# Attention stack on one core: sums one step later, two multiply-adds for the values, the shift in five GpSimd steps, 128 rows in the first stage

## The reference

```python
q = _fq_sym(q, axis=-1); k = _fq_sym(k, axis=-1); v = _fq_sym(v, axis=2)   # 127 levels
attn = jnp.einsum('bhqd,bhkd->bhqk', q, k)
attn = jax.nn.softmax(attn, axis=-1)
attn = _fq_unsigned(attn, axis=-1)         # s = max(attn) / 255; round(attn / s) * s
out = jnp.einsum('bhqk,bhkd->bhqd', attn, v)
return out @ Wp + bp
```

## Time and profile before

| | |
|---|---|
| time, median of 3 runs | 4641.71 us (4641.0 to 4643.88) |
| the profiled execution: its time, its span | 4639.28 us, 4636.2 us |
| TensorE, VectorE, ScalarE, GpSimd busy | 96%, 87%, 76%, 80% |
| first stage | 0 to about 730 us |
| heads 0 to 14 | about 730 to 3972 us, 226 us the first, then about 215 us each |
| last head, epilogue | to about 4197 us, to the end |
| TensorE's mean granted clock | 0.982 |

### The profile page before, as it was taken

How to read it: one execution, slowest core, us unless ns; L and a number is a source line. 1 busy time by engine, 2 the same in 40 slices (tenths; PEclk the granted TensorE clock), 3 DMA queues, 4 the chain that set the end, 5 groups by cost and what they waited for, 6 DMA issues and landing times. The chain is left out here.

```text
span 4636.2 us, 150451 instructions
## 1 busy us (share of the span) xinstructions
PE 4459.4 (96%) x54175; PEld 1971.5 (43%) x54175; DVE 4037.1 (87%) x7370; ACT 3531.4 (76%) x3643; POOL 3692.6 (80%) x4025
## 2 busy tenths in 40 slices
PE   7999998999999999999999999999999999888999
PEld 5666663333333333333333333333333333224665
DVE  6788888999999999999999999999999999774333
ACT  3555557889889898989898988989898989873121
POOL 5777776899999999999999999999999999772000
PEclk9999997999999999999999999999999999998999
DMA  3555542111111111111111111111111111442010
GB/s 101 150 164 161 171 148 66 35 35 33 35 33 34 35 34 35 33 34 34 33 35 35 32 36 33 34 35 35 34 33 35 34 33 32 144 155 91 0 38 8
DMA packets 222771, 268.77 MB, mean 58 GB/s; under 512 B 34366, under 2 KB 202809, under 8 KB 221289
## 3 DMA queue, kind: packets, MB, share of 16 engines
q1 hardware_dynamic: 167529, 203.57, 15.8%
q10 hardware_dynamic: 54528, 55.60, 3.8%
HBM read 174.57 MB, written 82.97 MB: 56 GB/s over the span
## 5 line engine op out<-in xcount | busy, mean ns | idle before, releaser
L1546 ACT ACTIVATE e_home<-ps_scores,sk 125x896 f32<-125x896 f32 x3072 | 3076.2, 1008 | 388.7 <-ACTq L1545 204.3
L1579 DVE TENSOR_REDUCE unit_max<-ps_maxima 128x1 f32<-128x428 f32 (+2 forms) x5760 | 3115.2, 607 | 54.4 <-DVEq L1576 40.9
L1764 POOL TENSOR_SCALAR r<-e_home 125x896 f32<-125x896 f32 x2976 | 2769.6, 954 | 287.1 <-ACT e_home L1546 114.7
L1349 PE MATMUL ps_maxima<-e_home,unit 125*17 125x224 f32 x24576 | 1705.7, 354 | 12.2 <-PEq L1333 7.6
L1321 PE MATMUL ps_maxima<-k_home,q 48*128 48x428 bf16 (+2 forms) x5760 | 1614.8, 350 | 15.8 <-issue 1.8
L1293 PE MATMUL ps_scores<-q,k_home 54*128 54x448 bf16 x5760 | 1592.7, 356 | 4.8 <-PEq L1468 2.9
L1341 PE MATMUL ps_maxima<-r,vt 125*16 125x224 f16 x12288 | 854.5, 267 | 60.8 <-PEq L1335 30.7
L1293 PEld LDWEIGHTS ps_scores<-q,k_home 54*128 54x128 bf16 x5760 | 329.6, 95 | 1064.0 <-issue 1034.7
L1341 PEld LDWEIGHTS ps_maxima<-r,vt 125*16 125x16 f16 x12288 | 300.3, 86 | 783.0 <-issue 780.7
L1349 PEld LDWEIGHTS ps_maxima<-e_home,unit 125*17 125x17 f32 x24576 | 620.0, 95 | 19.2 <-issue 17.0
L1321 PEld LDWEIGHTS ps_maxima<-k_home,q 48*128 48x128 bf16 x5760 | 524.2, 93 | 233.3 <-issue 63.7
(11 more groups left out here) (270 smaller groups left out, 2723.6 us busy)
## 6 DMA issues: line engine op xcount, KB each, us to landing
k_rows<-krows ACTq DMA_DIRECT2D x48, 1000.0 KB, 7.0
k_home<-k_rows SPq DMA_DIRECT2D x408, 93.8 KB
k_home<-k_rows SPq DMA_DIRECT2D x120, 281.2 KB
e_home<-in_ctxT SPq DMA_DIRECT2D x48, 500.0 KB, 4.2
vr<-v_raw SPq DMA_DIRECT2D x128, 187.5 KB
cb<-in_ctxT SPq DMA_DIRECT2D x16, 1500.0 KB, 6.1
v_raw<-e_home SPq DMA_DIRECT2D x12, 1000.0 KB
v_raw<-vb SPq DMA_DIRECT2D x12, 1000.0 KB
```

Of the source, the lines that this page charges most:

```text
L1349: made = pe.matmul(psav[c:c + WIDE, lo:hi], unit[:, :], e[(i + s) % SLOTS][0:KT, g, lo:hi], start=head_first and part == 0, stop=False, sk ...
L1546: act.activation(e[i % SLOTS][0:KT, :, :], score_banks(i)[0:KT, :, :], ACT.Exp, scale=sk[u][:, i:i + 1]).then_inc(e_wrote[h % 2], 1)
L1579: top = dve.tensor_reduce(maxima[y][:, b, slot:slot + 1], ps[:, 0:hi - lo], axis=AX.X, op=ALU.max)
L1764: pool.tensor_scalar(r[i % SLOTS][:, :, :], e[i % SLOTS][0:KT, :, :], 1.0, WHOLE_WORD, ALU.mult, ALU.add)\
```

## The change

Sums: `LAG` becomes 6 and the parity in `step_sums` turns, so that both parts of a pair stand one step later; one part more is issued behind the last step. Values: both multiplications without a wait, then one operation over all 24 tiles that multiplies by one and adds the large number (step 7), and one that multiplies by one and subtracts it (step 10). Shift: `turn_shift` has five parts, one behind each rounding of steps 13 to 17; a copy is written to several places at once, the scales are negated once ahead, and the 255 levels are no longer an addend of the shift but a factor in the roundings and in the weights of the exact sums. First stage: the bias, its ones and the queries of head 0 are tiles of 128 rows, filled up with zeros (bias, queries) or ones, and L511 and L556 run over 128 rows; the clearing is one memset on VectorE and one on GpSimd.

```diff
-LOG255 = math.log(255.0)
+LEVELS = 255.0
...
@@ head_max, high_part, other_parts
-        dve_done(dve.tensor_scalar(shift[:, :], shift[:, :], -1.0, LOG255, ALU.mult, ALU.add))
+    def shift_copies(n):
+
+        return shift[:, :].rearrange("p (b o) -> p b o", o=1).to_broadcast([QB, NQB, n])
+
+    HIGH, MID, LOW = slice(0, SROWS, 2), slice(1, SROWS - 1, 2), SROWS - 1
+    T_ROWS = ((0, 1, 5), (2, 3), (4,))
     def high_part():
-        dve_done(dve.tensor_copy(shift_parts[:, :, 0], shift[:, :]))
+        dve_done(dve.tensor_copy(shift_parts[:, :, HIGH], shift_copies(3)))
         dve_done(dve.tensor_tensor(shift[:, :], shift[:, :], shift_parts[:, :, 0], ALU.subtract))
     def other_parts():
-        dve_done(dve.tensor_copy(shift_parts[:, :, 1], shift[:, :]))
-        dve_done(dve.tensor_tensor(shift_parts[:, :, 2], shift[:, :], shift_parts[:, :, 1], ALU.subtract))
-        dve.tensor_copy(shift_parts[:, :, 3:5], shift_parts[:, :, 0:2])
-        dve.tensor_copy(shift_parts[:, :, 5], shift_parts[:, :, 0]).then_inc(shift_ready, 1)
+        dve_done(dve.tensor_copy(shift_parts[:, :, MID], shift_copies(2)))
+        dve.tensor_tensor(shift_parts[:, :, LOW], shift[:, :], shift_parts[:, :, 1], ALU.subtract)\
+           .then_inc(shift_ready, 1)
...
-        pool_done(pool.tensor_tensor(part, part,
...
+        pool.tensor_tensor(part, part,
+                           v_inv[:, bass.ds(h * HDIM, HDIM)].rearrange("p (o d) -> p o d", o=1)
+                           .to_broadcast([KT, VTILES, HDIM]), ALU.mult).then_inc(v_scaled, 1)
+
+    def raised_values():
+
+        pool.wait_ge(v_scaled, 2).then_inc(v_scaled, -2)
+        pool.tensor_scalar(vr[:, :, :], vr[:, :, :], 1.0, ROUND, ALU.mult, ALU.add).then_inc(v_raised, 1)
-    def whole_values(x, half):
-        tiles = slice(half * VTILES, (half + 1) * VTILES)
-        pool_done(pool.tensor_scalar(x[:, tiles, :], vr[:, tiles, :], ROUND, ROUND, ALU.add, ALU.subtract))
+    def whole_values(x):
+        pool.wait_ge(v_raised, 1).then_inc(v_raised, -1)
+        pool_done(pool.tensor_scalar(x[:, :, :], vr[:, :, :], 1.0, -ROUND, ALU.mult, ALU.add))
...
@@ first stage
-        bias = sbuf(st, "k_bias", [PARTS, 2 * DIM], bf16)
-        ones = sbuf(st, "k_ones", [PARTS, KT], bf16)
+        bias = sbuf(st, "k_bias", [P, 2 * DIM], bf16)
+        ones = sbuf(st, "k_ones", [P, KT], bf16)
...
-        q0 = sbuf(st, "q0", [HROWS, TOK], bf16)
+        q0 = sbuf(st, "q0", [P, TOK], bf16)
...
-                    pe.matmul(first_bank(n, b)[:, 0:GK], q0[:, b * QB:(b + 1) * QB],
-                              rows[n % 2][0:HROWS, DIM // P, :], start=True, stop=True, tile_position=(0, 0))\
-                      .then_inc(s_full, 1)
+                    pe.matmul(first_bank(n, b)[:, 0:GK], q0[:, b * QB:(b + 1) * QB], rows[n % 2][:, DIM // P, :],
+                              start=True, stop=True).then_inc(s_full, 1)
...
+            dve_done(dve.memset(bias[:, :], 0.0))
+            own = bias[0:PARTS, :]
...
+            dve.wait_ge(sq_landed, 16).then_inc(sq_landed, -16)
+            dve_done(dve.tensor_scalar(sq[:, :, :], sq[:, :, :], -1.0, None, ALU.mult))
...
+            pool_done(pool.memset(q0[:, :], 0.0))
+            pool.sem_inc(q0_cleared, 1)
...
-                for row in ((0, 1, 2), (3, 4), (5,))[r]:
+                for row in T_ROWS[r]:
...
@@ attention
-    LAG = 5
+    LAG = 6
...
-    SCALED, WHOLE, CHAINED = (1, 4), (SLOTS - 1, SLOTS + 2), 13
+    SCALED, RAISED, WHOLE, CHAINED = (1, 4), 7, 10, range(13, 18)
...
-                    at = i - LAG - (1 - i % 2)
+                    at = i - LAG - i % 2
...
-                        sums(at, u, 1 - i % 2, shared=not first)
+                        sums(at, u, i % 2, shared=not first)
...
+            sums(CT - 6, 1, 0, shared=True)
             last_exponentials(CT - 2)
...
+            def turn_shift(h1, part):
+
+                if part == 0:
+                    pool.wait_ge(max_ready, 1).then_inc(max_ready, -1)
+                    pool_done(pool.tensor_tensor(shift[:, :], run_max[:, :],
+                                                 sq[:, :, bass.ds(h1, 1)].rearrange("p b o -> p (b o)"), ALU.mult))
+                if part == 1:
+                    pool_done(pool.tensor_copy(shift_parts[:, :, HIGH], shift_copies(3)))
+                if part == 2:
+                    pool_done(pool.tensor_tensor(shift[:, :], shift[:, :], shift_parts[:, :, 0], ALU.subtract))
+                if part == 3:
+                    pool_done(pool.tensor_copy(shift_parts[:, :, MID], shift_copies(2)))
+                if part == 4:
+                    pool.tensor_tensor(shift_parts[:, :, LOW], shift[:, :], shift_parts[:, :, 1], ALU.subtract)\
+                        .then_inc(shift_ready, 1)
...
-                pool.tensor_scalar(r[i % SLOTS][:, :, :], e[i % SLOTS][0:KT, :, :], 1.0, WHOLE_WORD, ALU.mult, ALU.add)\
+                pool.tensor_scalar(r[i % SLOTS][:, :, :], e[i % SLOTS][0:KT, :, :], LEVELS, WHOLE_WORD, ALU.mult, ALU.add)\
                     .then_inc(r_ready, 1)
...
-            pool_done(pool.memset(unit[:, HDIM:], HALF_UNIT))
+            pool_done(pool.memset(unit[:, HDIM:], LEVELS * HALF_UNIT))
```

More of the change, by code:

```diff
@@ L905, in pool_program @@
                 scaled_values(0, half)
-                whole_values(vt0, half)
+            raised_values()
+            whole_values(vt0)
         def act_program():
@@ L1328, in sums @@
                 if (i, part) == (0, 0):
[L1329 removed]
+                    pe.wait_ge(vt_ready, 1).then_inc(vt_ready, -1)
                 if part == 0:
@@ L1457, in step_sums @@
                     elif at >= 0:
-                        sums(at, u, 1 - i % 2, shared=not first)
+                        sums(at, u, i % 2, shared=not first)
                     elif not head_start or finished is not None:
-                        sums(at + CT, 1 - u, 1 - i % 2, head_end=head_start and i == LAG - 1,
+                        sums(at + CT, 1 - u, i % 2, head_end=head_start and i == LAG - 1,
                              shared=not first and not head_start)
@@ L1747, in pool_program @@
         def pool_program():
-            def turn_shift(h1):
-                pool.wait_ge(max_ready, 1).then_inc(max_ready, -1)
-                pool_done(pool.tensor_tensor(shift[:, :], run_max[:, :],
-                                             sq[:, :, bass.ds(h1, 1)].rearrange("p b o -> p (b o)"), ALU.mult))
-                pool_done(pool.tensor_scalar(shift[:, :], shift[:, :], -1.0, LOG255, ALU.mult, ALU.add))
-                for part in range(2):
-                    pool_done(pool.tensor_copy(shift_parts[:, :, part], shift[:, :]))
-                    rest = shift[:, :] if part == 0 else shift_parts[:, :, 2]
-                    pool_done(pool.tensor_tensor(rest, shift[:, :], shift_parts[:, :, part], ALU.subtract))
-                pool_done(pool.tensor_copy(shift_parts[:, :, 3:5], shift_parts[:, :, 0:2]))
-                pool.tensor_copy(shift_parts[:, :, 5], shift_parts[:, :, 0]).then_inc(shift_ready, 1)
+            def turn_shift(h1, part):
[12 more added lines that the diff above has]
+                        .then_inc(shift_ready, 1)
             def rounded(n, i):
@@ L1771, in chunk @@
                         rounded(n, i)
-                    if n % NCH == NCH - 1 and i == CHAINED and n // NCH < HEADS - 1:
-                        turn_shift(n // NCH + 1)
+                    if n % NCH == NCH - 1 and i in CHAINED and n // NCH < HEADS - 1:
+                        turn_shift(n // NCH + 1, CHAINED.index(i))
                     if h is not None and i in SCALED:
                         scaled_values(h, SCALED.index(i))
-                    if h is not None and i in WHOLE:
-                        if i == WHOLE[0]:
-                            pool.wait_ge(v_free[1 - u], 1).then_inc(v_free[1 - u], -1)
-                        whole_values(vt[1 - u], WHOLE.index(i))
+                    if h is not None and i == RAISED:
+                        raised_values()
+                    if h is not None and i == WHOLE:
+                        pool.wait_ge(v_free[1 - u], 1).then_inc(v_free[1 - u], -1)
+                        whole_values(vt[1 - u])
             pool.sem_inc(v_free[1], 1)
```

23 lines of the change are left out of this document (10 added, 13 removed).

## The result

The changed kernel took 4728.35 us (median of 4, 4726.9 to 4740.14), the kernel before on the same chip 4642.8 us. The ratio is 1.0187 with a 95% interval of 1.0168 to 1.0207: 86 us slower, where 90 us faster were forecast, far outside the range 4510 to 4602.

A forecast was written before the change was run, and what follows sets the result against it. TensorE bounds the first stage, VectorE the heads; in the last head TensorE waits for roundings. Terms: -50 - 0.5 - 33 - 7 + 0.9 = -89.6 us, from 4641.7 to 4552 us; range 4510 to 4602.

The forecast's parts named there:

- Folding a constant into an operation that exists already: Heads: the multiplication by 255 moves from the shift into the rounding's scalar and the sums' weights; same instructions, nothing.
- the next engine's idle time: First stage: 128 rows relieve TensorE; 80% of VectorE's 41.5 us wait taken as gain, 33 us of the 50.

The follow-up runs named there:

- half the search: Kernel with only the 128 rows, VectorE's maxima of the values cut to two of four tiles of each generation: 4603.54 us (0.9902).

## What to carry to other kernels

Folding a constant into an operation that exists already is not free because the instruction count stays the same. Put one of the factors that ran cheap here into GpSimd's multiply-add (1, 2, 3, 129 or 256; another one has to be measured) and keep the rest of the constant where it is cheap; here a small operation once a head did it.

Read an engine's pace from start to start in a run of equal instructions, not from the mean duration, and write down for the engine next to the bound how much it has to spare per period. Here that was 1.6 us in 26, and 24 instructions share it: 0.07 us more on each is enough.

When the bound of a stage is relieved, don't book the next engine's idle time as gain. Price its operations again for running beside others; a cheap test is to make that next engine faster and look at what moves.

## What the hardware showed that I had not expected

- GpSimd's multiply-add with an immediate factor over 125x896 follows itself every 0.902 to 0.904 us with factors 1, 2, 3, 129 and 256, and every 1.017 to 1.020 us with 15, 127, 255 and 255/128; the duration shown is 0.94 us in all.
- The same instruction with one operation, an addition, takes 2.458 us.
- In the kernel after TensorE's granted clock fell to 0.50 at the end of each of heads 1 to 14, around a wait of some 4 us, and stayed there for 3.4 or 6.8 us.
- A bias operand makes ScalarE's activation over 125x896 longer by 91 ns.
- VectorE's operation on 32 scales took from 0.18 to 1.02 us with 128 rows (to 1.61 with half the search), and where it was long it ended 0.06 us behind a GpSimd operation. That is read from the traces and was not tried by an experiment of its own.
